# A last pass in which VectorE aggregates its statistics one round later, between product and addition, and ScalarE normalises three steps behind its exponential

## The chip, the cores and the metric

The kernel runs on one core of one Trainium2 chip. The metric is the device time of one execution in microseconds. A core has five engines with queues of their own: TensorE (PE), VectorE (DVE), ScalarE (ACT), GpSimd (POOL) and SyncE (SP), which here issues loads. Each works through its instructions in program order, and they meet at semaphores: an instruction may wait until a semaphore has reached a value, and may raise one when it is done. Sixteen DMA engines move data between HBM and the on-chip memories.

## The reference, cut to what matters

Four graph layers over 50000 nodes of 256 features, each followed by a residual and a layer norm. The last is a graph attention layer with 4 heads of 64:

```python
h = (x @ W.T).reshape(N, H, C)
...
alpha = p / (denom[dst] + 1e-16)
msg = alpha[:, :, None] * h[src]
out = jax.ops.segment_sum(msg, dst, num_segments=N)
out = out.reshape(N, H * C) + bias
out = jax.nn.elu(out) + x
```

and then, over each node's 256 features, the layer norm:

```python
m = jnp.mean(x, axis=axis, keepdims=True)
v = jnp.var(x, axis=axis, keepdims=True)
return (x - m) / jnp.sqrt(v + eps)
```

Each node is also its own neighbour (a loop edge), so every node has a term with `h` of its own.

## The kernel before

The program is a list of phases, with a barrier behind each. The last phase (`l_sync`, `l_scalar`, `l_gpsimd`, `l_vector`, `l_tensor`) makes one pass over all nodes. Phases ahead of it have put into the DRAM table `tab`, for every node, the weighted sum of its neighbours' messages with the bias, and the weight of its own term per head. The pass works in NS = 98 rounds of 512 nodes, 128 partitions with J = 4 nodes each. For round k:

- SyncE loads the layer's input `x3_d` (512 KB, `l_rows`, L1989, eight buffers `l_xt`) and the table rows (544 KB, `tables`, L1996, four buffers `l_tt`).
- TensorE transposes the input (`tr`, L2016, 8 instructions) and multiplies it with the weights (`mm`, L2025, 16 instructions into one of two pairs of PSUM banks). It transposes k+1 ahead of the products of k.
- ScalarE copies the transposed input to SBUF (`evac`, L2041, two instructions), takes the exponential into PSUM (`exps`, L2047; `l_un` has one buffer, so it waits for L2125 of the round before), then normalises (`normed`, L2054, four instructions, scale times value plus bias) and issues the store of 512 KB (`store`, L2061, four buffers `l_y`).
- VectorE multiplies TensorE's result with the weights of the own term, in PSUM (L2114, called the *product* below), and adds the table rows (L2118, the *addition*); both are in `weighted(k)`, and the addition waits for the product's semaphore. `unit(k-1)` is one instruction (L2125) that makes elu + 1 from sum and exponential. `stats(k-2)` issues four `bn_stats` (L2131, the *statistics*), waits for them, does a small memset (L2134) and four `bn_aggr` (L2136, the *aggregates*) into `l_mv`, one buffer of mean and variance.
- GpSimd adds the residual (`residual(k-1)`, L2084, into one of four buffers `l_rr`), then makes the *factors* 1/sqrt(var + eps) and -mean times that (`rstd(k-2)`, L2090 to L2096, four small instructions, two buffers).

`run_beats` runs the rounds: 8 written out ahead, 80 in a loop whose body has 8 rounds (ten turns), 10 written out behind. In the loop a wait's value is computed in registers (L90), and L68 is the loop's branch. No scheduler moves anything: on each engine the order of the calls in `body(k)` is the order of the instructions.

Of the kernel before, what the change touches and what calls it, by code (L numbers as in the profile page):

```python
# [57 lines left out]
def beat(s, period):  # L58
    return Beat(s, s % period, s // period, period)


def run_beats(eng, total, body, period, peel=4, tail=4, start=0):


    first, last = -(-(start + peel) // period), (start + total - tail) // period
    for s in range(start, period * first):
        body(beat(s, period))
    with eng.Fori(first, last) as m:  # L68
        for i in range(period):
            body(Beat(period * m + i, i, m, period))  # L70
    for s in range(period * last, start + total):
        body(beat(s, period))
# [12 lines left out]
def wait(eng, signal, value):  # L85

    if isinstance(value, int) and value <= 0:
        return
    if isinstance(signal, Signal):
        eng.wait_ge(signal.sem, signal.base + value)  # L90
    else:
        eng.wait_ge(signal, value)


def gnn_program(nc, x, src, dst, ea256, ea64,
# [20 lines left out]
    NS = -(-N // STEP)  # L116
# [29 lines left out]
    def node_view(t, k, cols=slice(None), start=0):  # L146

        if k.known() and k.s - start == NS - 1:
            a = t[(NS - 1) * STEP:N, cols].rearrange("(p j) d -> p j d", j=J)
            return a, NLAST  # L150
        a = t[0:(NS - 1) * STEP, cols].rearrange("(s p j) d -> s p j d", p=P, j=J)
        return a[k.s - start, :, :, :], P

    def live(k, total):
        return not (k.known() and k.s >= total)

    ctx = ExitStack()
    with ctx:
# [1801 lines left out]
        PER = 8  # L1960
# [75 lines left out]
        def l_scalar(act):  # L2036
            def evac(k):
                wait(act, lp["tr"], k.s + 1)
                wait(act, lp["mm"], k.s - 1)
                for f in range(FH):  # L2040
                    act.activation(l_xT[:, k.slot(2), f, :], l_tr[:, f, :], ACT.Copy).then_inc(lp["xT"].sem, 1)  # L2041

            def exps(k):

                wait(act, lp["t"], k.s + 1)
                wait(act, lp["u"], k.s)
                act.activation(l_un, l_sum[:, k.slot(2), :, :], ACT.Exp, bias=minus[:, 0:1]).then_inc(lp["ex"].sem, 1)  # L2047

            def normed(k):
                b = k.slot(4)  # L2050
                wait(act, lp["nm"], k.s + 1)
                wait(act, l_w[b], 16 * k.turn(4))
                for j in range(J):
                    act.activation(l_y[:, b, j, :], l_rr[:, b, j, :], ACT.Identity, bias=l_nm[:, k.slot(2), j:j + 1],  # L2054
                                   scale=l_rs[:, k.slot(2), j:j + 1]).then_inc(lp["y"].sem, 1)

            def store(k):
                b = k.slot(4)
                wait(act, lp["y"], J * (k.s + 1))
                a, n = node_view(out, k)  # L2060
                act.dma_start(a, l_y[0:n, b, :, :]).then_inc(l_w[b].sem, 16)  # L2061
            evac(beat(0, PER))
            evac(beat(1, PER))

            def body(k):
                if live(k.plus(2), NS):
                    evac(k.plus(2))
                exps(k)
                if not (k.known() and k.s < 3):
                    store(k.plus(-3))  # L2070
                if not (k.known() and k.s < 2):
                    normed(k.plus(-2))
            run_beats(act, NS, body, PER, peel=PER)
            store(beat(NS - 3, PER))
            normed(beat(NS - 2, PER))
            store(beat(NS - 2, PER))
            normed(beat(NS - 1, PER))
            store(beat(NS - 1, PER))
# [29 lines left out]
        def l_vector(v):  # L2108
            def weighted(k):
                b, c = k.slot(2), 2 + 2 * k.slot(2)  # L2110
                own = psum[:, c:c + 2, :]
                wait(v, lp["mm"], k.s + 1)
                wait(v, l_t[k.slot(NTT)], 16 * (k.turn(NTT) + 1))
                v.tensor_tensor(out=own.rearrange("p a (j h c) -> p (a j) h c", j=2, h=H3), in0=own.rearrange("p a (j h c) -> p (a j) h c", j=2, h=H3),  # L2114
                                in1=l_tt[:, k.slot(NTT), :, WC3:WC3 + H3].rearrange("p j (h a) -> p j h a", a=1).to_broadcast([P, J, H3, HD3]),
                                op=ALU.mult).then_inc(lp["pr"].sem, 1)
                wait(v, lp["pr"], k.s + 1)
                v.tensor_tensor(out=l_sum[:, b, :, :], in0=own.rearrange("p a (j d) -> p (a j) d", j=2), in1=l_tt[:, k.slot(NTT), :, 0:D],  # L2118
                                op=ALU.add).then_inc(lp["t"].sem, 1)

            def unit(k):

                wait(v, lp["ex"], k.s + 1)
                wait(v, lp["r"], k.s - 1)
                v.scalar_tensor_tensor(out=l_pr[:, k.slot(2), :, :], in0=l_un, scalar=1.0, in1=l_sum[:, k.slot(2), :, :], op0=ALU.min, op1=ALU.max).then_inc(lp["u"].sem, 1)  # L2125

            def stats(k):
                wait(v, lp["r"], k.s + 1)
                wait(v, lp["mv"], J * k.s)
                for j in range(J):  # L2130
                    v.bn_stats(l_st[:, j, :], l_rr[:, k.slot(4), j, :]).then_inc(lp["st"].sem, 1)  # L2131
                wait(v, lp["st"], J * (k.s + 1))
                wait(v, lp["ve"], 2 * k.s)
                v.memset(l_gap, 0.0)  # L2134
                for j in range(J):
                    v.bn_aggr(l_mv[:, j, :], l_st[:, j, :]).then_inc(lp["mv"].sem, 1)  # L2136

            def body(k):
                weighted(k)
                if not (k.known() and k.s < 1):  # L2140
                    unit(k.plus(-1))
                if not (k.known() and k.s < 2):
                    stats(k.plus(-2))
            run_beats(v, NS, body, PER, peel=PER)
            unit(beat(NS - 1, PER))
            stats(beat(NS - 2, PER))
            stats(beat(NS - 1, PER))

        PHASES.append((e2_sync, e2_scalar, e2_gpsimd, e2_vector, e2_tensor))
        PHASES.append((e3_sync, e3_scalar, e3_gpsimd, e3_vector, e3_tensor))  # L2150
        PHASES.append((l_sync, l_scalar, l_gpsimd, l_vector, l_tensor))

        def everything(eng, which):
# [48 lines left out]
```

## Time and profile before

| | us |
|---|---|
| median of 3 runs | 5101.81 (5099.42 to 5104.55) |
| the profiled execution, its own time | 5100.59 |
| its span | 5098.9 |
| product of round 0 to product of round 97 | 4553.39 to 5075.02 |

The span is what the profile's records cover. The last pass is about a tenth of it; everything ahead of the pass is the same in both kernels. In a timeline row the first number is the start in us from the span's start, the second the time that the group of equal instructions (x4 and so on) took in all; brackets say how long the engine had been idle ahead of it and who released it.

### The profile page before, as it was taken

What the parts mean: (1) busy time and instruction counts of PE and PEld (TensorE: products, weight loads), DVE (VectorE), ACT (ScalarE), POOL (GpSimd) and SP (SyncE); (2) the same over time, 40 slices, a digit from 0 to 9 for tenths busy, and PEclk for the clock granted to TensorE, in tenths of its full rate; (3) what the DMA queues carried; (4) which work ended last, traced back from release to release, by engine and by line L of the source; (5) the groups of instructions that cost most, each with busy time, mean ns of one, the idle gap of its engine ahead of it and who ended that gap; (6) DMA issues with size and microseconds to landing.
All of it is one profiled execution on the core that took longest, in us unless ns stands there. A gap on an engine that the chain in (4) does not pass through costs nothing. (4 is left out here: it accounts for less than half of the span.)

```text
span 5098.9 us, 69926 instructions
## 1 busy us (share of the span) xinstructions
PE 4199.0 (82%) x18336; PEld 3042.4 (60%) x18336; DVE 3509.5 (69%) x10200; ACT 1961.3 (38%) x3445; POOL 3218.7 (63%) x3078
## 2 busy tenths in 40 slices
PE   2177759998999999999999999766676687768886
PEld 1055535555666666666666666555566576767675
DVE  3055546666666666666666666599999688879998
ACT  0011115553333333333333333344444222237776
POOL 7388754444456666666566665677776677757776
PEclk6589879999999999999999999888877788889999
DMA  9988879998544444444444444255554444448886
GB/s 374 324 157 154 161 140 361 364 367 318 192 172 155 143 141 139 139 144 143 142 143 149 148 147 141 101 182 182 191 187 171 132 138 138 139 165 297 296 296 229
DMA packets 449380, 994.26 MB, mean 195 GB/s; under 512 B 147560, under 2 KB 230474, under 8 KB 449198
## 3 DMA queue, kind: packets, MB, share of 16 engines
q1 hardware_dynamic: 296146, 732.73, 42.3%
q0 software_dynamic: 100736, 172.47, 13.6%
q10 hardware_dynamic: 52316, 87.06, 5.1%
q8 instruction: 62, 1.02, 0.1%
q14 instruction: 120, 0.98, 0.1%
HBM read 493.48 MB, written 541.33 MB: 203 GB/s over the span
## 5 line engine op out<-in xcount | busy, mean ns | idle before, releaser
L1140 PE MATMUL psum<-W2b,arena 128*128 128x256 f32 x3136 | 725.2, 379 | 0.0
L1121 PE MATMUL psum<-arena,W1b 128*128 128x512 f32 x1568 | 699.1, 599 | 0.0
L1140 PEld LDWEIGHTS psum<-W2b,arena 128*128 128x128 f32 x3136 | 573.1, 190 | 66.3 <-issue 0.5
L1121 PEld LDWEIGHTS psum<-arena,W1b 128*128 128x128 f32 x1568 | 289.8, 190 | 402.8 <-issue 402.8
L1009 ACT ACTIVATE arena<-psum,hbias 128x512 f32<-128x512 f32 x392 | 269.5, 688 | 559.2 <-PE psum L1121 559.2
L825 DVE TENSOR_SCALAR arena<-arena 128x256 f32<-128x256 f32 x392 | 135.2, 408 | 439.2 <-POOL arena L820 439.2
L1367 PE MATMUL psum<-Wg,arena 128*128 128x264 f32 x784 | 275.6, 485 | 195.4 <-ACT arena L1402 183.8
L959 POOL DMA_INDIRECT xd_d<-arena,FE x360 | 356.7, 991 | 99.3 <-issue 99.3
L464 POOL DMA_INDIRECT tab<-arena x196 | 311.3, 1588 | 167.0 <-DMA tab<-zero 67.8
L816 POOL TENSOR_TENSOR arena<-arena,lneps 128x4 f32<-128x4 f32 x196 | 41.9, 214 | 553.1 <-DVE arena L812 552.3
L603 PE MATMUL psum<-arena,NEG 128*128 128x324 f32 x500 | 178.2, 523 | 247.6 <-ACT arena L409 214.9
L1097 PE MATMUL psum<-W2a,arena 128*128 128x256 f32 x1568 | 357.2, 381 | 9.3 <-ACT arena L995 9.3
L2025 PE MATMUL psum<-Wg,arena 128*128 128x256 f32 x1568 | 355.7, 380 | 0.6 <-ACT arena L2041 0.6
L1097 PEld LDWEIGHTS psum<-W2a,arena 128*128 128x128 f32 x1568 | 299.5, 191 | 92.7 <-issue 54.4
L778 PE MATMUL psum<-arena,W1a 128*128 128x512 f32 x784 | 354.3, 595 | 0.0
L728 POOL DMA_INDIRECT fe_d<-EID,FIRST x196 | 196.6, 1003 | 239.7 <-ACT arena L753 203.1
L939 POOL TENSOR_TENSOR arena<-arena,b2b 128x1024 f32<-128x1024 f32 x98 | 230.8, 2355 | 156.8 <-DVE arena L1078 153.8
L2084 POOL TENSOR_TENSOR arena<-arena 128x1024 f32<-128x1024 f32 x98 | 230.5, 2352 | 148.3 <-DVE arena L2125 135.9
L1071 DVE TENSOR_TENSOR arena<-arena 128x4 f32<-128x4 f32 x98 | 214.5, 2188 | 149.7 <-issue 146.8
L409 ACT ACTIVATE arena<-psum 128x324 f32<-128x324 f32 x196 | 71.5, 445 | 631.8 <-DMA tab<-arena 578.7
L2025 PEld LDWEIGHTS psum<-Wg,arena 128*128 128x128 f32 x1568 | 291.0, 191 | 36.7 <-ACT arena L2041 1.0
L1367 PEld LDWEIGHTS psum<-Wg,arena 128*128 128x128 f32 x784 | 169.3, 239 | 235.8 <-ACT arena L1402 195.3
(349 smaller groups left out, 10141.8 us busy)
## 6 DMA issues: line engine op xcount, KB each, us to landing
arena<-in_x SPq DMA_DIRECT2D x194, 512.0 KB, 5.6
x_d<-arena SPq DMA_DIRECT2D x194, 512.0 KB, 3.6
tab<-zero SPq DMA_DIRECT2D x11, 5832.0 KB, 55.1
arena<-x_d SPq DMA_DIRECT2D x105, 512.0 KB, 4.7
tab<-blank SPq DMA_DIRECT2D x97, 544.0 KB
arena<-tab SPq DMA_DIRECT2D x97, 544.0 KB, 5.3
h_d<-arena SPq DMA_DIRECT2D x98, 512.0 KB, 4.7
arena<-h_d SPq DMA_DIRECT2D x98, 512.0 KB
```

Of the source, the lines that this page charges most:

```text
L464: pool.indirect_dma_start(out=tab0[:, :], out_offset=bass.IndirectOffsetOnAxis(ap=sidx[:, s, j:j + 1], axis=0), in_=comb[:, s % NC, j, :], ...
L778: last = pe.matmul(psum[:, 4 + 2 * b + g, :], W1a[:, f, g * P:(g + 1) * P], hT[:, b, f, :], start=(f == 0), stop=(f == FH - 1))
L939: pool.tensor_tensor(out=x1b[:, k.b, :, :], in0=x1[:, k.b, :, :], in1=b2b[:, :].rearrange("p (a d) -> p a d", a=1).to_broadcast([P, J, D]) ...
L959: pool.indirect_dma_start(out=xd_d[:, :], out_offset=bass.IndirectOffsetOnAxis(ap=FE[:, s * J + j:s * J + j + 1], axis=0), in_=x2[:, s % 2 ...
L1009: act.activation(hid[:, c, :], psum[:, HB[c], :], ACT.Relu, bias=hbias[:, c:c + 1]).then_inc(p3["hidr"], 1)
L1071: v.tensor_tensor(out=lone[:, 0, :], in0=lnB.mv[:, :, 1], in1=lnB.rs, op=ALU.mult).then_inc(lonely["lvar"], 1)
L1097: last = pe.matmul(outA(j), p3y[:, f, j * P:(j + 1) * P], W2a[:, f, :], start=(f == 0), stop=(f == FH - 1))
L1121: last = pe.matmul(psum[:, HB[c], :], W1b[:, f, c * P:(c + 1) * P], x1T[:, f, :], start=False, stop=(f == FH - 1))
L1140: last = pe.matmul(outB(j), hid[:, c, j * P:(j + 1) * P], W2b[:, c, :], start=(c == 0), stop=(c == KH - 1))
L1367: pe.matmul(o[:, 0:D + H2], xT2[:, j % 2, f, :], Wg[2][:, f, 0:D + H2], start=(f == 0), stop=(f == FH - 1))
L2025: done = pe.matmul(psum[:, c + j // 2, (j % 2) * D:(j % 2 + 1) * D], l_xT[:, k.slot(2), f, j * P:(j + 1) * P], Wg[3][:, f, 0:D], start=(f ...
L2084: pool.tensor_tensor(out=l_rr[:, k.slot(4), :, :], in0=l_pr[:, k.slot(2), :, :], in1=l_xt[:, k.slot(NXT), :, :], op=ALU.add).then_inc(lp[" ...
```

## The change

`stats` is cut in two: the `bn_stats` stay, and the wait for them, the memset and the `bn_aggr` become `moments`. `moments(k-3)` is called inside `weighted(k)`, between the product and the addition. Before, the aggregates of round k-2 stood at the end of body k; now they stand behind product k+1. On ScalarE the normalisation and the store go one round later: `normed(k-3)` and `store(k-4)` in place of `normed(k-2)` and `store(k-3)`. GpSimd's code is as before: `rstd(k-2)` in body k, behind `residual(k-1)`.

```diff
--- before.py
+++ after.py
@@ -2066,11 +2066,13 @@
                 if live(k.plus(2), NS):
                     evac(k.plus(2))
                 exps(k)
+                if not (k.known() and k.s < 4):
+                    store(k.plus(-4))
                 if not (k.known() and k.s < 3):
-                    store(k.plus(-3))
-                if not (k.known() and k.s < 2):
-                    normed(k.plus(-2))
+                    normed(k.plus(-3))
             run_beats(act, NS, body, PER, peel=PER)
+            store(beat(NS - 4, PER))
+            normed(beat(NS - 3, PER))
             store(beat(NS - 3, PER))
             normed(beat(NS - 2, PER))
             store(beat(NS - 2, PER))
@@ -2114,6 +2116,8 @@
                 v.tensor_tensor(out=own.rearrange("p a (j h c) -> p (a j) h c", j=2, h=H3), in0=own.rearrange("p a (j h c) -> p (a j) h c", j=2, h=H3),
                                 in1=l_tt[:, k.slot(NTT), :, WC3:WC3 + H3].rearrange("p j (h a) -> p j h a", a=1).to_broadcast([P, J, H3, HD3]),
                                 op=ALU.mult).then_inc(lp["pr"].sem, 1)
+                if not (k.known() and k.s < 3):
+                    moments(k.plus(-3))
                 wait(v, lp["pr"], k.s + 1)
                 v.tensor_tensor(out=l_sum[:, b, :, :], in0=own.rearrange("p a (j d) -> p (a j) d", j=2), in1=l_tt[:, k.slot(NTT), :, 0:D],
                                 op=ALU.add).then_inc(lp["t"].sem, 1)
@@ -2129,6 +2133,8 @@
                 wait(v, lp["mv"], J * k.s)
                 for j in range(J):
                     v.bn_stats(l_st[:, j, :], l_rr[:, k.slot(4), j, :]).then_inc(lp["st"].sem, 1)
+
+            def moments(k):
                 wait(v, lp["st"], J * (k.s + 1))
                 wait(v, lp["ve"], 2 * k.s)
                 v.memset(l_gap, 0.0)
@@ -2142,9 +2148,12 @@
                 if not (k.known() and k.s < 2):
                     stats(k.plus(-2))
             run_beats(v, NS, body, PER, peel=PER)
+            moments(beat(NS - 3, PER))
             unit(beat(NS - 1, PER))
             stats(beat(NS - 2, PER))
+            moments(beat(NS - 2, PER))
             stats(beat(NS - 1, PER))
+            moments(beat(NS - 1, PER))
 
         PHASES.append((e2_sync, e2_scalar, e2_gpsimd, e2_vector, e2_tensor))
         PHASES.append((e3_sync, e3_scalar, e3_gpsimd, e3_vector, e3_tensor))
```

On VectorE, the first round behind the loop; in brackets `rows_in0` is the table rows' load, `p2_mm` TensorE's products, `l_pr` the product, `e2_ex` the exponential, `e2_r` GpSimd's residual, `lnA_st` the statistics, `lnA_mv` the aggregates, `lnA_ve` GpSimd's reading of them. Before:

```order
L2114 TENSOR_TENSOR psum<-psum,arena 128x1024 [waits rows_in0,p2_mm]
L2118 TENSOR_TENSOR arena<-psum,arena 128x1024 [waits l_pr]
L2125 SCALAR_TENSOR_TENSOR arena<-psum,arena 128x1024 [waits e2_r,e2_ex]
L2131 BN_STATS arena<-arena 128x6 [waits lnA_mv,e2_r]
L2131 BN_STATS arena<-arena 128x6 x3
L2134 MEMSET arena 128x2 [waits lnA_ve,lnA_st]
L2136 BN_AGGR arena<-arena 128x2 x4
```

And on VectorE in the same place now:

```order
L2116 TENSOR_TENSOR psum<-psum,arena 128x1024 [waits rows_in0,p2_mm]
L2140 MEMSET arena 128x2 [waits lnA_ve,lnA_st]
L2142 BN_AGGR arena<-arena 128x2 x4
L2122 TENSOR_TENSOR arena<-psum,arena 128x1024 [waits l_pr]
L2129 SCALAR_TENSOR_TENSOR arena<-psum,arena 128x1024 [waits e2_r,e2_ex]
L2135 BN_STATS arena<-arena 128x6 [waits lnA_mv,e2_r]
L2135 BN_STATS arena<-arena 128x6 x3
```

Memset and aggregates have moved from behind the statistics to behind the next round's product; the product now follows the statistics, and the addition the aggregates. In the loop, the body has register instructions (L90) in between. On VectorE, a round of the loop's body before:

```order
L2114 TENSOR_TENSOR psum<-psum,arena 128x1024 [waits rows_in2]
L90 REGISTER_ALU
L2118 TENSOR_TENSOR arena<-psum,arena 128x1024 [waits l_pr]
L90 REGISTER_ALU
L2125 SCALAR_TENSOR_TENSOR arena<-psum,arena 128x1024 [waits e2_r,e2_ex]
L2131 BN_STATS arena<-arena 128x6 [waits lnA_mv,e2_r]
L2131 BN_STATS arena<-arena 128x6 x3
L90 ISA
L90 ISA [waits lnA_st]
L2134 MEMSET arena 128x2 [waits lnA_ve]
L2136 BN_AGGR arena<-arena 128x2 x4
```

And on VectorE, the same round of the loop's body now:

```order
L2116 TENSOR_TENSOR psum<-psum,arena 128x1024 [waits rows_in2]
L90 ISA
L90 ISA [waits lnA_st]
L2140 MEMSET arena 128x2 [waits lnA_ve]
L2142 BN_AGGR arena<-arena 128x2 x4
L90 REGISTER_ALU
L2122 TENSOR_TENSOR arena<-psum,arena 128x1024 [waits l_pr]
L90 REGISTER_ALU
L2129 SCALAR_TENSOR_TENSOR arena<-psum,arena 128x1024 [waits e2_r,e2_ex]
L2135 BN_STATS arena<-arena 128x6 [waits lnA_mv,e2_r]
L2135 BN_STATS arena<-arena 128x6 x3
```

The wait for the statistics, with its register instruction, has moved along with the memset. On ScalarE, rounds 2 and 3, written out ahead of the loop (`l_t` is the addition's semaphore, `e2_u` that of L2125, `e2_nm` GpSimd's factors, `lnA_y` the normalisation, `p2_tr` the transposes). Before:

```order
L2047 ACTIVATE psum<-arena,minus 128x1024 [waits e2_u,l_t]
L2054 ACTIVATE arena<-arena 128x256 [waits e2_nm]
L2054 ACTIVATE arena<-arena 128x256 x3
L2041 ACTIVATE arena<-psum 128x512 [waits p2_mm,p2_tr]
L2041 ACTIVATE arena<-psum 128x512
L2047 ACTIVATE psum<-arena,minus 128x1024 [waits e2_u,l_t]
L2061 DMA out_x<-arena 128x1024 [waits lnA_y]
L2054 ACTIVATE arena<-arena 128x256 [waits e2_nm]
```

And on ScalarE in rounds 2 and 3 now:

```order
L2047 ACTIVATE psum<-arena,minus 128x1024 [waits e2_u,l_t]
L2041 ACTIVATE arena<-psum 128x512 [waits p2_mm,p2_tr]
L2041 ACTIVATE arena<-psum 128x512
L2047 ACTIVATE psum<-arena,minus 128x1024 [waits e2_u,l_t]
L2054 ACTIVATE arena<-arena 128x256 [waits e2_nm]
L2054 ACTIVATE arena<-arena 128x256 x3
```

The first normalisation stands one round later, behind the exponential of round 3 instead of that of round 2, and the first store a round later too; the order within a round is the same.

## Rows read from the trace of the kernel before

**Rows 1.** Windows, the loop of the pass: busy us and instructions of each engine.
```profile
core 0: us, PE busy (x) PEld busy (x) DVE busy (x) ACT busy (x) POOL busy (x), PEclk, DMA share, GB/s
4593.51:5027.82 434.31, 363.82 (x1920) 302.90 (x1920) 415.42 (x961) 323.58 (x562) 310.28 (x401) 1.00 0.89 296
```

**Rows 2.** Waits in the loop: who waited <- for whom: us, times, longest.
```profile
ACT arena L2054 <- POOL arena L2096: 110.7, 80, 1.9
...
POOL arena L2084 <- DVE arena L2125: 99.8, 71, 1.9
...
DVE arena L2134 <- DVE arena L2131: 10.6, 65, 0.2
```

**Rows 3.** Timeline of an unrolled round, VectorE's instructions in it.
```profile
5054.06 1.21 DVE L2114 TENSOR_TENSOR psum<-psum,arena 128x1024 f32<-128x1024 f32 x1
...
5057.57 1.40 DVE L2131 BATCH_NORM_STATS2 arena<-arena 128x6 f32<-128x256 f32 x4
...
5059.01 0.18 DVE L2136 BATCH_NORM_AGGREGATE arena<-arena 128x2 f32<-128x6 f32 x1
...
5059.30 1.21 DVE L2114 TENSOR_TENSOR psum<-psum,arena 128x1024 f32<-128x1024 f32 x1
```

**Rows 4.** Timeline of one round in the loop, VectorE.
```profile
4642.40 1.21 DVE L2114 TENSOR_TENSOR psum<-psum,arena 128x1024 f32<-128x1024 f32 x1
4643.65 1.22 DVE L2118 TENSOR_TENSOR arena<-psum,arena 128x1024 f32<-128x1024 f32 x1
4644.79 1.21 DVE L2125 SCALAR_TENSOR_TENSOR arena<-psum,arena 128x1024 f32<-128x1024 f32 x1
4645.92 1.39 DVE L2131 BATCH_NORM_STATS2 arena<-arena 128x6 f32<-128x256 f32 x4
4647.48 0.06 DVE L2134 MEMSET arena<- 128x2 f32 x1 [0.16 <-DVE arena L2131]
...
4647.77 1.21 DVE L2114 TENSOR_TENSOR psum<-psum,arena 128x1024 f32<-128x1024 f32 x1
```

**Rows 5.** Timeline, VectorE, the product behind the loop's branch.
```profile
4680.47 1.23 DVE L2114 TENSOR_TENSOR psum<-psum,arena 128x1024 f32<-128x1024 f32 x1 [0.34 <-issue]
```

**Rows 6.** Instructions of L90, VectorE's sequencer: ns min/median/max, first and last start.
```profile
L90 DVEq FUSED_REGOPS  x1: 53/53/53, 4644.1 to 4644.1; - x1
```

**Rows 7.** Timeline, products of rounds 0, 2, 3 and 97.
```profile
4553.39 1.23 DVE L2114 TENSOR_TENSOR psum<-psum,arena 128x1024 f32<-128x1024 f32 x1 [12.86 <-PE psum L2025]
...
4561.99 1.23 DVE L2114 TENSOR_TENSOR psum<-psum,arena 128x1024 f32<-128x1024 f32 x1 [0.71 <-PE psum L2025]
...
4567.26 1.21 DVE L2114 TENSOR_TENSOR psum<-psum,arena 128x1024 f32<-128x1024 f32 x1
...
5075.02 1.21 DVE L2114 TENSOR_TENSOR psum<-psum,arena 128x1024 f32<-128x1024 f32 x1
```

**Rows 8.** Timeline, all engines, from a VectorE round's start in the loop.
```profile
4799.69 1.22 DVE L2114 TENSOR_TENSOR psum<-psum,arena 128x1024 f32<-128x1024 f32 x1
...
4803.38 2.35 POOL L2084 TENSOR_TENSOR arena<-arena 128x1024 f32<-128x1024 f32 x1 [1.34 <-DVE arena L2125]
...
4805.01 1.11 ACT L2047 ACTIVATE psum<-arena,minus 128x1024 f32<-128x1024 f32 x1
...
4807.21 0.20 POOL L2096 TENSOR_TENSOR arena<-arena 128x4 f32<-128x4 f32 x1
...
4807.54 2.07 ACT L2054 ACTIVATE arena<-arena 128x256 f32<-128x256 f32 x4 [1.43 <-POOL arena L2096]
...
4809.52 0.57 ACT L2041 ACTIVATE arena<-psum 128x512 f32<-128x512 f32 x1
...
4811.56 3.62 PE L2025 MATMUL psum<-Wg,arena 128*128 128x256 f32 x16
```

**Rows 9.** Windows: unrolled rounds of the pass, and a stage far ahead of it.
```profile
4580.00:4596.00 16.00, 13.89 (x75) 11.61 (x74) 15.77 (x38) 12.13 (x21) 11.61 (x16) 1.00 0.89 303
...
892.00:1020.00 128.00, 128.00 (x479) 69.85 (x478) 77.28 (x90) 73.17 (x119) 57.65 (x60) 1.00 1.02 364
```

## The prediction, written before the changed kernel ran

> **What bounds the kernel now.** I read the profile from the last pass's stretches down to single instructions. The windows table [rows 1] gives the loop of the pass: its eighty rounds take 434.31 us, 5.43 each. VectorE works 415.42 us of that, 96%; TensorE, ScalarE and GpSimd have 84%, 75% and 71%, TensorE's granted clock is 1.00 (the 2.4 GHz level) and the DMA share is 0.89. The waits of the same stretch [rows 2] say who follows whom: GpSimd waits 100 us for VectorE in 71 rounds, ScalarE 111 us for GpSimd in all 80; VectorE's own largest wait is 10.6 us, for its own statistics. So the others wait in a row that begins at VectorE, and the question is what a VectorE round consists of.
>
> The unrolled rounds at the end [rows 3] are 5.24 apart: product to statistics 3.51, statistics to aggregates 1.44, aggregates to next product 0.29. The round in the loop [rows 4] has, start to start, product to addition 1.25, addition to L2125 1.14, L2125 to statistics 1.13, statistics to memset 1.56, memset to next product 0.29: 5.37. Two of these steps are longer than the work needs. Addition to L2125 is 1.14 though the addition runs 1.22: an instruction whose waits have long been met starts 0.08 before the end of the one ahead. The addition waits for the product directly ahead of it and starts 0.04 behind its end: 0.12 lost. The memset waits for the statistics directly ahead, which run 1.39 and could be followed after 1.31: 0.25 lost in the loop, where register instructions stand behind the wait, 0.13 in the unrolled rounds. Once in eight rounds the loop's branch comes on top: the product starts after 0.34 of idle time [rows 5] instead of 0.08 early, 0.42 in all, because the sequencer sat in the wait for the statistics and came to the branch only then.
>
> **What the change takes away.** No arithmetic is added or removed. (a) The aggregates of round k-3 stand between product k and addition k. Their statistics were issued in round k-1, so that wait is met when the product has just begun; by the 1.14 of an instruction with met waits the memset follows the product after 1.14. (b) Memset and four aggregates keep their 0.29 [rows 3, 4]. In today's loop they are followed by a product with two waits and two register instructions, still after 0.29; the addition has one wait, which is met during the aggregates. I take 0.29, with 0.12 more as the upper bound. (c) Addition to L2125 1.14, L2125 to statistics 1.13. (d) Statistics to next product 1.39 - 0.08 = 1.31. Sum 1.14 + 0.29 + 1.14 + 1.13 + 1.31 = 5.01.
>
> (e) In the loop, are registers and branch hidden? The sequencer's row [rows 6] says that it runs far ahead: the register instruction that the code has behind the four statistics executes at 4644.1, while the addition of 4643.65 still runs and 3.4 us before the memset of 4647.48 [rows 4]. So L2125 and four statistics were queued by then. In the new order the sequencer is held by the product's semaphore until the addition, and from there it has 3.6 us of queued work before the next product; branch and registers lie under it. I take 5.015 in the loop too and 0 for the branch. Uncovered, the branch costs 0.42 x 10 = 4 us, and 0.04 more in every round 4 us.
>
> Sum over the pass. Rounds 0 and 1 (8.60 together) are paced by TensorE's first products and stay. Round 2 loses its aggregates, 5.27 [rows 7] to 4.82. The other 94 intervals take 94 x 5.015 = 471.4. First to last product is then 8.60 + 4.82 + 471.4 = 484.8 us, against 5075.02 - 4553.39 = 521.63 today [rows 7]: 36.8 less. Behind the last product GpSimd's last rounds hang on the L2125 of that round, which now has the aggregates ahead of it and no gap behind the product: 1.14 + 0.29 + 1.14 = 2.57 against 2.39, so the tail grows by 0.2. Net 36.6.
>
> **Who could be late next.** I follow time from the start of product k in the new order; the durations are in [rows 8]. *GpSimd*: L2125 ends at 2.57 + 1.21 = 3.8, the residual runs 3.9 to 6.2. The factors of k-2 wait for the aggregates in round k+1, at 5.01 + 1.14 + 0.4 = 6.55, and take 1.7 (residual's end at 4805.73 to 4807.41), to 8.3; the next residual is due at 8.9. Margin 0.6, and behind that 2.5 until VectorE's statistics want the residual. *ScalarE*: its exponential waits for L2125 of k-1, which frees the PSUM banks: 3.9 to 5.0. The factors of k-3 are ready at 3.3, so the normalisation starts at once and runs its 2.07 to 7.0, two evacuations to 8.1; the next exponential is due at 8.9. That is what three steps buy. With two steps today's chain runs from L2125 (2.4 behind the product of 4799.69) over residual 4803.38, factors, normalisation 4807.54, evacuations 4809.52, transposes, to the products' end, 4811.56 + 3.62 = 4815.18, and they are wanted by the product three rounds on: (4815.18 + 0.1 - 4799.69) / 3 = 5.2 a round. Had only VectorE's order changed, this chain would bind near today's pace. In the new order TensorE, 4.6 behind the evacuations' end, is done at 12.7 and wanted at 15.03; its own work is 4.6 a round. The store keeps its place directly ahead of the normalisation, so a buffer of y still has three rounds in which to be stored. *SyncE's* two loads wait for addition and residual as before, 4 and 7 rounds ahead.
>
> *DMA*: a round moves 1568 KB, and 0.89 x 5.43 = 4.83 us of it is transfer. At 5.01 that would be 320 GB/s and 96%. Yet unrolled rounds at 5.24 move 303 GB/s at the same share, 0.89 x 5.24 = 4.66 us a round, so a transfer gets no dearer with the pace, and another stage of this kernel holds 364 GB/s for 128 us [rows 9]. I cost it at nothing, with a rival below.
>
> **A rule that speaks against it.** The trace shows the two dependent pairs starting 0.12 and 0.25 later than a pair whose waits are met [rows 4]; the sum rests on that. The Trainium skill, "VectorE: DVE Perf Modes", section "The DRAIN you can't avoid", states that the next operation waits until the pipe is empty in any case and that a semaphore between two costs nothing extra; its section "Rules for kernel authors" says to save operations, not semaphores. By that rule the round would stay as it is and the sum be 0; the starts 0.08 before an end do not agree with it.
>
> **Rivals.** *R1, waits still cost in their new places* (5%): product to memset 1.24 instead of 1.14, and the addition 0.12 behind the aggregates. Round 5.23: 434.31 - 80 x 5.23 = 15.9, with 1 from the unrolled rounds 17 less, 5085. For it: both waits are met only shortly before; against: shortly is 1.1 and 0.2 us. *R2, DMA paces it* (5%): the rate stops at that of the unrolled rounds, 5.24: 434.31 - 80 x 5.24 = 15.1, and 3.5 from the others: 19 less, 5083. For it a share of 0.89, against it rows 9. *R3, no gain* (6%): what a dependent pair loses is the emptying of the pipe, which shows again between the new neighbours (a memset behind a 1024-wide operation, a product behind statistics); 5.37 stays, 5102. The rule above would give this. *R4, slower* (4%): every wait costs its register time where it stands: 0.25 ahead of the memset, 0.12 ahead of the addition and, since the product's waits now stand behind the statistics, the 0.34 of rows 5 in each round: 5.01 + 0.71 = 5.72, 80 x 0.29 = 23 more, 5125. It turns into a loss when the three together pass 0.42 a round. Against it: L2125, with two waits and registers ahead of it, starts after 1.14. The forecast has 80%.
>
> **How the numbers follow.** The profiled execution took 5100.59 (span 5098.9 and 1.7 around it); minus 36.6 is 5064.0. The median of the runs is 1.2 above it: 5065.2, say 5065.5. The likeliest case's own range: down to 5062 (runs of before lie 2.6 apart from the median), up to 5074 (branch uncovered and 0.04 a round). For 8 in 10 a little is added on either side, to 5060 and, towards R1 and R2, to 5080. 0.2% is 10 us, about what a measurement tells from no change: faster 0.90 (forecast, R1, R2), same 0.06 (R3), slower 0.04 (R4).
>
> **What would show it.** Right: products 5.01 to 5.03 apart in loop and unrolled rounds alike, without the long eighth; memset 1.14 behind the product, addition 0.29 behind it, the next product 1.31 behind the statistics; no idle time of VectorE put down to its statistics; ScalarE idle ahead of the exponential, not ahead of the normalisation; DMA share near 0.94. Wrong: a memset 1.24 or later behind the product (R1, R4); VectorE waiting for TensorE or for a table load (R2, or a ScalarE chain longer than I reckoned); a residual that starts later than 0.1 behind L2125's end, which would say that the late factors hold it up.

## The result, and the profile after

| | before | after |
|---|---|---|
| median of 4 runs, us | 5102.47 (5099.42 to 5104.55) | 5057.72 (5055.26 to 5064.78) |
| ratio of the runs, 95% interval | | 0.9918 (0.9902 to 0.9933) |
| the profiled execution, its own time | 5100.59 | 5059.13 |
| its span | 5098.9 | 5057.4 |
| product of round 0 to product of round 97 | 521.63 | 481.02 |
| from the last product to the span's end | 23.88 | 24.07 |

Faster, and by a little more than forecast: the medians lie 44.8 us apart, the profiled executions 41.5, and the interval of the ratio is 34 to 50 us. The median came out 2.3 us below the forecast's range. The part of the trace that the change touches is known better than that: 40.6 us less between the first and the last product, 0.2 more behind the last one.

The products' rows in the timeline of the kernel after, rounds 0, 2, 3 and 97, which answer to [rows 7]:

```profile
4552.31 1.23 DVE L2116 TENSOR_TENSOR psum<-psum,arena 128x1024 f32<-128x1024 f32 x1 [12.58 <-PE psum L2025]
...
4560.91 1.23 DVE L2116 TENSOR_TENSOR psum<-psum,arena 128x1024 f32<-128x1024 f32 x1 [0.71 <-PE psum L2025]
4565.76 1.22 DVE L2116 TENSOR_TENSOR psum<-psum,arena 128x1024 f32<-128x1024 f32 x1
...
5033.33 1.29 DVE L2116 TENSOR_TENSOR psum<-psum,arena 128x1024 f32<-128x1024 f32 x1
```

Round 2 takes 4.85 instead of 5.27; from round 3 on all 94 intervals are 4.97 or 4.98, in the loop and outside it, and the long eighth round [rows 5] is gone. One round of the timeline after, VectorE, answers to [rows 3, 4]:

```profile
4640.38 1.23 DVE L2116 TENSOR_TENSOR psum<-psum,arena 128x1024 f32<-128x1024 f32 x1
4641.51 0.26 DVE L2142 BATCH_NORM_AGGREGATE arena<-arena 128x2 f32<-128x6 f32 x2
4641.61 0.06 DVE L2140 MEMSET arena<- 128x2 f32 x1
4641.67 0.23 DVE L2142 BATCH_NORM_AGGREGATE arena<-arena 128x2 f32<-128x6 f32 x2
4641.80 1.21 DVE L2122 TENSOR_TENSOR arena<-psum,arena 128x1024 f32<-128x1024 f32 x1
...
4642.90 1.23 DVE L2129 SCALAR_TENSOR_TENSOR arena<-psum,arena 128x1024 f32<-128x1024 f32 x1
...
4644.04 1.41 DVE L2135 BATCH_NORM_STATS2 arena<-arena 128x6 f32<-128x256 f32 x4
...
4645.35 1.23 DVE L2116 TENSOR_TENSOR psum<-psum,arena 128x1024 f32<-128x1024 f32 x1
```

Start to start 1.13, 0.29, 1.10, 1.14, 1.31 (the aggregates' first record taken as the start of their group): the next instruction begins about 0.1 before the end of the one ahead. The memset is the exception. The code issues it ahead of the aggregates, yet its record starts 1.23 behind the product, when the product's record ends, and after the first aggregate's. So the 1.13 and the 0.29 can't be told apart with certainty; product to addition is 1.42 together. The windows (4600 to 5000) and the waits (4600 to 4990) of a stretch in the loop, of the kernel after, answer to [rows 1, 2]:

```profile
4600.00:5000.00 400.00, 365.62 (x1931) 304.53 (x1930) 400.00 (x970) 328.17 (x565) 315.64 (x401) 1.00 0.93 323
```

```profile
ACT psum L2047 <- DVE arena L2129: 70.9, 79, 0.9
...
POOL arena L2086 <- DVE arena L2129: 41.0, 79, 0.6
PE psum L2016 <- ACT arena L2041: 33.4, 78, 0.5
POOL arena L2092 <- DVE arena L2142: 29.3, 78, 0.4
```

VectorE is busy 400.00 of 400 us and has no row among the waits. ScalarE's idle time has moved to the exponential, where the prediction looked for it, and fell from 1.4 to 0.9 us a round. DMA goes along at 323 GB/s and a share of 0.93.

### The profile page after: what moved, and what is told of

Its sections match the earlier page's. It is cut to its first block and busy times, and to the rows that moved or that the text cites. A ratio compares the mean times of both kernels' runs of the same rounds, so it can differ in the third digit from the quotient of the medians.

```text
span 5057.4 us, 69936 instructions
## 1 busy us (share of the span) xinstructions
PE 4217.5 (83%) x18336; PEld 3058.7 (60%) x18336; DVE 3491.4 (69%) x10200; ACT 1965.0 (39%) x3445; POOL 3222.5 (64%) x3078
## 5 line engine op out<-in xcount | busy, mean ns | idle before, releaser
L1367 PE MATMUL psum<-Wg,arena 128*128 128x264 f32 x784 | 300.3, 521 | 174.9 <-ACT arena L1402 174.9
L816 POOL TENSOR_TENSOR arena<-arena,lneps 128x4 f32<-128x4 f32 x196 | 41.5, 212 | 553.0 <-DVE arena L812 552.1
L603 PE MATMUL psum<-arena,NEG 128*128 128x324 f32 x500 | 167.7, 498 | 233.4 <-ACT arena L409 200.5
L2025 PE MATMUL psum<-Wg,arena 128*128 128x256 f32 x1568 | 355.4, 380 | 0.4 <-ACT arena L2041 0.4
L2025 PEld LDWEIGHTS psum<-Wg,arena 128*128 128x128 f32 x1568 | 290.8, 191 | 36.4 <-ACT arena L2041 0.8
L1367 PEld LDWEIGHTS psum<-Wg,arena 128*128 128x128 f32 x784 | 182.8, 258 | 212.7 <-ACT arena L1402 186.3
L1001 ACT ACTIVATE arena<-psum 128x512 f32<-128x512 f32 x196 | 117.1, 597 | 464.5 <-PE psum L1104 463.0
```

The costliest lines, as they stand in the source:

```text
L1367: pe.matmul(o[:, 0:D + H2], xT2[:, j % 2, f, :], Wg[2][:, f, 0:D + H2], start=(f == 0), stop=(f == FH - 1))
L2025: done = pe.matmul(psum[:, c + j // 2, (j % 2) * D:(j % 2 + 1) * D], l_xT[:, k.slot(2), f, j * P:(j + 1) * P], Wg[3][:, f, 0:D], start=(f ...
```

## Experiments

Each was run beside the kernel before, in two series: the first four beside runs of before with a median of 5097.72 us (20 runs), the others beside 5098.51 (10 runs). The expectations were worked out from 5102, so a median is to be compared by its ratio. Besides the ratio, each is read by the time from its first to its last product in one profile. That is the better measure here: the stages ahead of the pass are the same code in all of them, and yet the first product starts anywhere from 4543.92 (`unit` ahead of the addition) to 4554.34 us (no memset), a scatter of 10 us in code that the edits leave alone.

### Only VectorE's half

```diff
-                if not (k.known() and k.s < 4):
-                    store(k.plus(-4))
                 if not (k.known() and k.s < 3):
-                    normed(k.plus(-3))
+                    store(k.plus(-3))
+                if not (k.known() and k.s < 2):
+                    normed(k.plus(-2))
             run_beats(act, NS, body, PER, peel=PER)
-            store(beat(NS - 4, PER))
-            normed(beat(NS - 3, PER))
```

> Only VectorE's half of the change: aggregates of k-3 between product and addition, ScalarE as before (normalisation two steps behind its exponential). Theory: both halves are needed, because ScalarE's evacuations stand behind the normalisation in its queue. From the changed kernel's rows: product 4640.38, factors ready 4643.70 (3.3 behind it), normalisation 2.07, evacuations 1.05, transposes and products 4.61 behind them: the products of k+3 are there 11.1 behind product k+1, wanted by product k+3, two rounds on: 5.56 a round instead of 4.97. First to last product 8.6 + 4.9 + 94 x 5.56 = 536, 15 more than before: about 5117, VectorE idle ahead of the product for TensorE. Rival (the prediction's text): the chain binds near the pace of before, 5.2 a round: about 5080. Second rival: VectorE's order alone brings the whole gain, 4.97 a round, 5060.

Measured: 5116.82 us, ratio 1.0039 (1.0024 to 1.0053), slower than before. First to last product 540.2 us. The timeline of this kernel, one pair of rounds (line numbers are this kernel's):

```profile
4700.31 1.23 DVE L2114 TENSOR_TENSOR psum<-psum,arena 128x1024 f32<-128x1024 f32 x1 [0.89 <-PE psum L2025]
...
4703.44 0.20 POOL L2096 TENSOR_TENSOR arena<-arena 128x4 f32<-128x4 f32 x1
...
4703.77 2.07 ACT L2054 ACTIVATE arena<-arena 128x256 f32<-128x256 f32 x4 [2.00 <-POOL arena L2096]
...
4705.51 1.23 DVE L2114 TENSOR_TENSOR psum<-psum,arena 128x1024 f32<-128x1024 f32 x1
4705.75 0.57 ACT L2041 ACTIVATE arena<-psum 128x512 f32<-128x512 f32 x1
...
4707.79 3.62 PE L2025 MATMUL psum<-Wg,arena 128*128 128x256 f32 x16
...
4711.53 1.23 DVE L2114 TENSOR_TENSOR psum<-psum,arena 128x1024 f32<-128x1024 f32 x1 [0.94 <-PE psum L2025]
```

The chain can be walked: product 4700.31, factors ready 4703.64, normalisation, evacuation behind it in ScalarE's queue, TensorE's products done at 4711.41, product two rounds on at 4711.53. That is 11.22 for two rounds, 5.61 each, where 5.56 was expected; the rounds alternate, the short ones 5.0 to 5.4 and the long ones 5.9 to 6.2. Both rivals fell, the 5.2 of the prediction's text among them.

### Only ScalarE's half

The kernel before, with `store(k.plus(-4))` and `normed(k.plus(-3))` on ScalarE as in the change, and VectorE untouched.

> Only ScalarE's half: normalisation three steps behind the exponential, store with it, VectorE as before. Theory: VectorE bounds both, so its rounds stay 5.24 unrolled and 5.37 in the loop with 5.8 at each turn: 5102, within 3 us; ScalarE's idle time moves from the normalisation to the exponential. Rival: part of the gain came from ScalarE's order: rounds below 5.3 in the loop and less than 5095.

Measured: 5094.59, ratio 0.9996 (0.9986 to 1.0005). The median lies more than 3 us from the expected 5102 and just below the rival's 5095, but in this series the kernel before has 5097.72 and not 5102. What decides is the pass: first to last product 521.7 against 521.63, rounds 5.24, 5.38 and 5.80 as before. The rival fell. The waits of this kernel, 4600 to 4980:

```profile
ACT psum L2047 <- DVE arena L2127: 94.9, 70, 1.8
```

ScalarE now waits ahead of the exponential, and nobody gains by it. ScalarE's half is worth nothing alone; it is what keeps VectorE's half from a loss.

### One of the two savings taken back

```diff
-                if not (k.known() and k.s < 3):
-                    moments(k.plus(-3))
...
                     unit(k.plus(-1))
+                if not (k.known() and k.s < 3):
+                    moments(k.plus(-3))
                 if not (k.known() and k.s < 2):
                     stats(k.plus(-2))
```

with two buffers of statistics, and `stats` waiting for the aggregates of one round earlier.

> The changed kernel with the aggregates of k-3 one place further on, between L2125's instruction and the statistics (two buffers of statistics), so that the addition follows the product directly again while the wait for the statistics stays met. It takes back one of the two savings. Theory (each dependent pair costs by itself): product to addition 1.25 again, aggregates 0.29 elsewhere, so 0.12 to 0.14 a round more than the changed kernel: 5.10 a round, 12 us more, about 5070; the loop's branch stays hidden. Rival: the waits cost nothing and the gain came from the wait for the statistics alone: 4.97 a round, 5058.

Measured: 5068.02, ratio 0.9947 (0.9930 to 0.9963). First to last product 493.9 us, 12.9 more than the changed kernel. The timeline of this kernel, VectorE, one round:

```profile
4699.08 1.21 DVE L2116 TENSOR_TENSOR psum<-psum,arena 128x1024 f32<-128x1024 f32 x1
4700.33 1.23 DVE L2120 TENSOR_TENSOR arena<-psum,arena 128x1024 f32<-128x1024 f32 x1
4701.47 1.21 DVE L2127 SCALAR_TENSOR_TENSOR arena<-psum,arena 128x1024 f32<-128x1024 f32 x1
4702.61 0.18 DVE L2140 BATCH_NORM_AGGREGATE arena<-arena 128x2 f32<-128x6 f32 x1
...
4702.90 1.37 DVE L2133 BATCH_NORM_STATS2 arena<-arena 128x6 f32<-128x256 f32 x4
4704.19 1.22 DVE L2116 TENSOR_TENSOR psum<-psum,arena 128x1024 f32<-128x1024 f32 x1
```

Rounds of 5.11, each 0.14 longer: product to addition is 1.25 again. All rounds are alike, so branch and registers stay hidden as long as the wait for the statistics is met. Since ScalarE's half gains nothing alone, this kernel is also the measurement of the other saving by itself: with the wait for the statistics met and the product's wait exposed, the pass is 521.63 - 493.91 = 27.7 us shorter than before. Here the factors come over 2 us later within the round than in the changed kernel, which is more than the margin of 0.6 that the prediction gave GpSimd's residual. The residual does start late: L2127 ends at 4702.68, the residual follows at 4704.74, directly behind the last factor. VectorE still waits for nobody, because the residual ends at 4707.10 and its statistics start at 4708.01: the second margin, of 2.5 in the prediction, takes the delay.

### The other saving alone, with another cover

```diff
+                if not (k.known() and k.s < 1):
+                    unit(k.plus(-1))
                 wait(v, lp["pr"], k.s + 1)
                 v.tensor_tensor(out=l_sum[:, b, :, :], ...
...
                 weighted(k)
-                if not (k.known() and k.s < 1):
-                    unit(k.plus(-1))
```

on the kernel before; statistics, aggregates and ScalarE as before.

> The kernel before with another instruction as the cover: L2125 of k-1 stands between product k and addition k, statistics and aggregates as before, ScalarE as before. It takes the other saving alone. Theory: addition directly behind L2125 with its wait met, so unrolled rounds 5.24 - 0.12 = 5.12, in the loop 5.25 and the turn of 0.43 stays: 95 x 0.12 = 11 us less than before, 5091. Rival (a semaphore between two costs nothing): 5102. Second rival: the exponential, which now has to be there 1.1 earlier in the round, is late: VectorE idle ahead of L2125, slower than 5102.

Measured: 5082.86, ratio 0.9975 (0.9965 to 0.9985). First to last product 508.7 us, 12.9 less than before. The timeline of this kernel, VectorE, with a turn of the loop at the end:

```profile
4704.72 1.21 DVE L2114 TENSOR_TENSOR psum<-psum,arena 128x1024 f32<-128x1024 f32 x1
4705.84 1.21 DVE L2127 SCALAR_TENSOR_TENSOR arena<-psum,arena 128x1024 f32<-128x1024 f32 x1
4706.97 1.21 DVE L2120 TENSOR_TENSOR arena<-psum,arena 128x1024 f32<-128x1024 f32 x1
4708.10 1.39 DVE L2133 BATCH_NORM_STATS2 arena<-arena 128x6 f32<-128x256 f32 x4
...
4710.37 1.23 DVE L2114 TENSOR_TENSOR psum<-psum,arena 128x1024 f32<-128x1024 f32 x1 [0.34 <-issue]
```

Product to addition with L2127 (L2125's instruction) between them is two steps, 1.12 and 1.13; nothing is added for the dependence, and the turn's 0.34 stays. VectorE has no wait for ScalarE in 4600 to 4980, so the exponential comes in time, and both rivals fell. The saving is 0.13 a round with an instruction of 1.21 as the cover. What goes is the cost of an addition that waits for the instruction directly ahead of it. Whether that cost is the semaphore's or the dependence's own can't be told: in all these kernels each wait guards a result that is really needed.

### A memset as the cover

The kernel with the aggregates ahead of the statistics, and

```diff
+                v.memset(l_cov[:, k.slot(2), :], 0.0)
                 wait(v, lp["pr"], k.s + 1)
```

> As e3_aggregates_behind_unit (aggregates of k-3 ahead of the statistics, 5.11 a round), with one more memset of 2 values between product and addition. Asks what the 0.12 between a dependent pair is. Theory: time from the product's end to the arrival of its semaphore, so a cover shorter than 0.12 hides only itself: product to addition stays 1.25, round 5.11. Rival A: it is a price of being neighbours, which any instruction between takes away: product to addition 1.19, round 5.05. Rival B: the memset comes on top: 1.31, round 5.17.

Measured: 5074.98 in a single run; first to last product 493.9 us, the same as without it. The timeline of this kernel, VectorE:

```profile
4699.76 1.22 DVE L2117 TENSOR_TENSOR psum<-psum,arena 128x1024 f32<-128x1024 f32 x1
4700.98 0.06 DVE L2120 MEMSET arena<- 128x2 f32 x1
4701.01 1.23 DVE L2122 TENSOR_TENSOR arena<-psum,arena 128x1024 f32<-128x1024 f32 x1
```

Product to addition stays 1.25. A short cover costs nothing and saves nothing: the addition starts 0.03 to 0.04 behind the product's end, with the memset between them or with nothing. Both rivals fell. The four aggregates, 0.29, are long enough; 0.06 isn't.

### Without the memset in the unrolled rounds

```diff
-                v.memset(l_gap, 0.0)
+                if not k.known():
+                    v.memset(l_gap, 0.0)
```

> The changed kernel without the small memset ahead of the aggregates in the 18 rounds that are written out; the 80 rounds of the loop keep it. Read from the spacing of the products, unrolled against loop, in one profile. Theory: the memset takes its issue slot, about 0.06 us, so unrolled rounds 4.91 to 4.93 and loop rounds 4.97. Rival: it lies in the shadow of its neighbours, 4.97 in both.

Measured: 5060.99 in a single run. Unrolled rounds 4.96, loop rounds 4.97: the rival holds, the memset costs about 0.01 a round.

### Sixteen rounds in the loop's body

`PER = 16` in place of `PER = 8`, on the kernel before and on the changed one.

> The kernel before with 16 rounds in the loop's body in place of 8: four turns and 64 rounds in the loop, 34 written out. Theory: each turn costs VectorE 0.43 and each round in the loop 0.13 over an unrolled one, since its sequencer sits in the wait for the statistics: 6 turns less are 2.6, 16 rounds unrolled 2.1: 4.7 us less from first to last product (517 against 521.6). Rival: the long round at the turn is something else (fetching the body's code): it gets longer with the body, or stays every eighth round.

> The changed kernel with 16 rounds in the loop's body. Theory: turn and registers are already hidden, products stay 4.97 apart everywhere and first to last product 481, within 0.3. Rival: something of the loop is still paid: 1 us or more less.

Measured: before with 16, 5116.75, ratio 1.0037 (1.0026 to 1.0049), first to last product 543.1; changed with 16, 5069.16, ratio 0.9941 (0.9924 to 0.9958), 492.6. Both expectations were wrong, by 26 and 11.5 us; the rival of the first, that the long round gets longer with the body, held. Most rounds inside and outside the loop have the lengths of their kernels (5.38 and 5.24, 4.98). In the changed kernel, two rounds at each of the three turns take 6.4 to 7.3. In the timeline of the changed kernel with 16, VectorE, and the rows of L68 (the branch) in the same place:

```profile
4708.92 1.23 DVE L2116 TENSOR_TENSOR psum<-psum,arena 128x1024 f32<-128x1024 f32 x1 [1.66 <-issue]
...
4712.20 1.23 DVE L2122 TENSOR_TENSOR arena<-psum,arena 128x1024 f32<-128x1024 f32 x1 [1.75 <-issue]
```

```profile
L68 DVEq COMPARE_BRANCH  x1: 63/63/63, 4704.0 to 4704.0; - x1
L68 DVEq FUSED_REGOPS  x1: 63/63/63, 4708.7 to 4708.7; - x1
```

The branch is executed at 4704.0, well ahead of the product that would have been due at 4707.2, and the next instruction of the sequencer follows 4.7 us later. A second stop stands behind it where there is no branch: the addition starts at 4712.20, 1.75 us after the aggregates have ended. In the changed kernel with 8 rounds the same two rows of L68 are 0.3 us apart:

```profile
L68 DVEq COMPARE_BRANCH  x1: 62/62/62, 4627.3 to 4627.3; - x1
L68 DVEq FUSED_REGOPS  x1: 63/63/63, 4627.6 to 4627.6; - x1
```

From one branch to the next the trace has 324 records of VectorE with 16 rounds and 164 with 8, semaphore waits and register instructions among them. So the turn has two prices: the branch itself, hidden when the sequencer is ahead, and with the larger body stops of microseconds that a lead of 3 us does not hide.

The DMA rows of the same kernel say what the stops may be. Between 4640 and 4980 they have a queue of kind "instruction":

```profile
q14 instruction: 23, 0.19, 0.2%
q8 instruction: 3, 0.05, 0.1%
```

The two kernels with 8 rounds have no packet of that kind in the same stretch, so they repeat the body from its second pass on without any. With 16 rounds two such packets lie between 4704 and 4708.7, in the first gap, and one between 4710 and 4712.2, at the start of the second; at the other two turns too each of the two gaps has at least one, in it or at its start. That the stops are the fetching of code is therefore well supported, though the rows do not say which engine a packet is for. The Trainium skill, "Runtime: NRT & Kernel Launch", section "Instruction fetch mechanics", states that a taken branch whose target has left a window of two pages of 256 instructions waits until the page is fetched. The two traces agree with it in that the smaller body is not fetched again and the larger one is; at which size it begins no run here shows, and ScalarE's branch, with 259 records from one to the next, has no such gap (4706.8 to 4707.1).

The kernel before with 16 rounds loses more, and not only at the turn (there its product waits 4.1 us). Seven later rounds are 1.1 to 1.6 us longer because VectorE waits for TensorE, 8.2 us in all. The first of them, in the timeline of this kernel:

```profile
4730.52 1.97 PE L2016 MATMUL psum<-ident,arena 128*128 128x128 f32 x8 [4.74 <-ACT arena L2041]
4732.28 4.89 PE L2025 MATMUL psum<-Wg,arena 128*128 128x256 f32 x16
...
4737.21 1.23 DVE L2114 TENSOR_TENSOR psum<-psum,arena 128x1024 f32<-128x1024 f32 x1 [1.53 <-PE psum L2025]
```

TensorE had stood idle for 4.74 us behind the stop. In the windows table its granted clock is 0.60 between 4727 and 4732, a mean over both levels (1.2 and 2.4 GHz), where it is 1.00 (the 2.4 GHz level) from 4640 to 4700, and the 16 instructions of L2025 take 4.89 us in place of 3.62.

## Why the prediction was right

**The bound.** VectorE's rounds set the pace, and two waits on its own results made them longer than its work. The two savings show one by one: 12.9 us for the product's wait (taken back in one kernel, taken alone in the other), and 27.7 us for the wait on the statistics with what follows it, registers and branch (the kernel with the aggregates ahead of the statistics against before). Together they are the 40.6 that were measured.

**(a), (c), (d), the steps.** Expected 1.14, 1.14, 1.13 and 1.31; measured 1.13, 1.10, 1.14 and 1.31. **(b)** 0.29 expected and measured, nothing added for the addition's wait. In (a) the prediction spoke of the memset, 1.14 behind the product, and named "1.24 or later" as a sign of R1 or R4. By its own record the memset stands 1.23 behind the product, and only the first aggregate 1.13, so that sign could not tell the cases apart. What does is the step from product to addition: 1.42 measured, 1.43 predicted, 1.65 by R1. The sum was 5.01 and came out 4.97. Most of the 0.04 is addition to L2125: it is 1.14 wherever the addition follows its own wait, in the kernel before and in the two with the aggregates ahead of the statistics, and 1.10 behind the aggregates, where it starts before the end of the instruction ahead. The step was carried over from a place where the addition is entered differently; why it then takes 0.04 less was not tried. So the one term of the sum that was mis-sized is addition to L2125, taken as 1.14: 94 x 0.04 = 3.8 us is the whole of what the pass was off by, 484.8 predicted, 481.02 measured.

**(e), registers and branch.** Hidden. The branch of the kernel after is executed at 4627.3, 3.1 us ahead of the product of 4630.43; the prediction reckoned with 3.6 us of queued work. The long round before comes nine times, not ten, since nothing is repeated behind the last body: an uncovered branch would have been 3.8 us, not 4.

**The tail.** 0.2 more expected, 0.2 measured.

**Who could be late next.** Nobody. GpSimd waits 0.51 us ahead of the residual where a margin of 0.6 was reckoned. ScalarE's part held, with one error: that VectorE's order alone would "bind near today's pace", 5.2 a round. The prediction took today's chain, from L2125 of k-1 to the product three rounds on. With the aggregates behind product k+1 the chain begins there and has only two rounds: 5.61, slower than before by 19 us in the pass. The forecast did not rest on it, but it understated what the second half of the change is for.

**DMA.** Free, as costed: 0.93 of the share at 323 GB/s, where 0.94 and 320 were expected.

**The rivals.** R1 and R4 priced waits that have become easy to meet; they fall with 1.42 from product to addition and 1.31 from statistics to product. R2 falls with 4.97 a round; its sum had also counted 3.5 us from unrolled rounds that by its own rate would not have become shorter. R3 falls with the two kernels that only move the cover between product and addition: 12.9 us either way. The Trainium skill states ("VectorE: DVE Perf Modes", "The DRAIN you can't avoid") that a semaphore between two operations costs nothing extra; a wait on the instruction directly ahead costs 0.12 to 0.13 us in these traces. The prediction gave that section as saying that the next operation waits for an empty pipe "in any case"; the section also says that an operation which is not held starts earlier, and the starts about 0.1 before an end agree with that.

**The range.** It was too narrow. Runs of the same kernel before, in the two series beside the experiments, lay between 5090.70 and 5108.28 (20 and 10 runs), not within 2.6 of the median as the prediction had it of three runs (they lie up to 2.7 from it). The mechanism's part was sized within 4 us of 40. Of the 7.8 us between forecast and median 3.8 are the pass; 1.1 is the first product, which starts that much earlier in the profiled execution after than before (4552.31 against 4553.39). The remaining 2.9 come of putting the median 1.5 above the profiled execution, where it lies 1.4 below; that is within the scatter of runs, and no trace shows where in the program it arises.

## What to carry to other kernels

On an engine that is the bound, look for instructions that wait for the one directly ahead: in the timeline they are the pairs whose starts lie further apart than those of a pair with met waits (here 1.25 against 1.13, and 1.56 against 1.31). Put independent work between them that is long enough (0.29 and 1.21 were here, 0.06 was not), and then walk the chain of whatever you have made later, through the in-order queues of the other engines and back, counting how many rounds it has: it may need a step of its own, and here one half without the other was a loss.

Long instructions in front of the loop's branch hid it here only where no unmet wait held the sequencer ahead of it; and unrolling a body further can cost more than the branches it saves.

## What was not expected of the hardware

- A gap of 4.7 us between the branch and the next instruction of VectorE's sequencer with a body of 324 records, 0.3 us with 164, and a second stop of 1.75 us behind it with no branch near; instruction packets lie in both. It costs 11.5 us over three turns in the changed kernel, and more in the kernel before.
- The product of round 0 starts anywhere in 10 us (4543.92 to 4554.34) in kernels whose code ahead of the pass is the same.
- A memset of 2 values behind the product starts when the product's record ends (1.22 with the addition behind it, 1.23 with the aggregates), where an instruction of 1024 starts after 1.13; it delays nothing behind it.
